# Weighted sums of chunk 8 issued with those of chunks 9 to 11, with three exponential buffers

## Chip, core and metric

One Trainium2 chip, one of its NeuronCores. The metric is the device time of one execution in microseconds (us). The time before is the median of three runs. Engines: TensorE (PE; its weight loads PEld), VectorE (DVE), ScalarE (ACT), GpSimd (POOL), SyncE (SP, which issues the transfers).

## What is computed

A decoder layer for 32 sequences of 56 tokens with 128 features: self-attention (softmax over the query axis, then the upper triangle), layer norm; cross-attention to a context of 1500 rows of 96 features with 16 heads of 8 features; layer norm; a mixture of 8 experts; layer norm. The change is in the cross-attention:

```python
q = (query @ Wq + bq).reshape(B, Nq, H, D).transpose(0, 2, 1, 3)       # 32, 16, 56, 8
k = (key_value @ Wk + bk).reshape(B, Nkv, H, D).transpose(0, 2, 1, 3)  # 32, 16, 1500, 8
v = (key_value @ Wv + bv).reshape(B, Nkv, H, D).transpose(0, 2, 1, 3)
attn = jnp.einsum('bhqd,bhkd->bhqk', q, k) * scale
attn = jax.nn.softmax(jnp.clip(attn, -CLAMP, CLAMP), axis=-1)
x = jnp.einsum('bhqk,bhkd->bqhd', attn, v).reshape(B, Nq, Cq)
```

## The kernel before

Each engine has its own program, written out by hand; they meet at semaphores alone. The cross-attention takes one batch after another. A batch is a period of twelve slots, one for each chunk of 125 of its 1500 context rows (`NC` = 12), and in the slots of batch b other work for the batches b+1 and b+2 is interleaved, by tables at the top of the file. In slot c TensorE issues, in this order:

- the scores of chunk c of batch b (line 1056, four matmuls into two banks): context rows by 16 heads x 56 queries. It needs the exponential of chunk c-2, which frees the two banks;
- the maximum pieces of `EARLY_PIECES` (line 1042): a batch has 21 pieces of 128 (head, query) rows by 500 context rows, from which VectorE takes the maxima (line 738). Piece 0 has a bank of its own, the others alternate between two, so piece n waits until VectorE has reduced piece n-2 (line 1040). Pieces 0 to 8 are those of batch b+2 and stand in slots 8 to 11, the others those of batch b+1;
- in slot 0 the sum of weights of the batch before, spread over the rows (line 1069); in slots 9, 11 and 3 values (line 1081), in slots 5, 6 and 8 keys (line 1090), all through one bank that ScalarE empties (lines 587, 588 and 571);
- the pieces of `MID_PIECES`, in slot 8 the transpose of the maxima (line 1094);
- the weighted sums listed for the slot in `OUTPUTS` (lines 1096 to 1112): a chunk k is eight small products of its exponentials with its values (lines 1106 and 1110; the trace has two matmuls for each), written to strips of 32 rows of one bank. A chunk's sum waits for its exponential (line 1103) and counts up `outputs_made`;
- the pieces of `LATE_PIECES`.

In slots 8 to 11 the pieces are: 0 and 1 in slot 8, 2 and 3 in slot 9, 4 and 5 in slot 10 (before and behind the sums), 6, 7 and 8 in slot 11 (8 behind the sums).

ScalarE takes in slot c the exponential of chunk c (line 561) into one of three buffers (`NP` = 3). Buffer c mod 3 held chunk c-3, so that it first waits for that chunk's sum, and then makes its other copies of the slot; in slot 0 the copy of the finished sums (line 556) goes ahead of the exponential:

```python
act.wait_ge(F["scores_made"], b * NC + (c + 1) + PRIME)
if not (isinstance(b, int) and b == 0 and c < NP):
    act.wait_ge(F["outputs_made"], b * NC + (c + 1 - NP) + PRIME)
```

VectorE reduces the pieces in their order and between them does the small steps of the softmax (reciprocals, line 765; scaling, line 770; a check sum, line 775). SP moves keys, queries' extra rows and context between the buffers; POOL spreads queries and makes the low parts of the keys. Batches -2 to 1 and 28 to 32 are written out, the others are a loop of two batches.

Of the kernel before, what the change touches and what calls it, by code (L numbers as in the profile page):

```python
# [51 lines left out]
EARLY_PIECES = {0: (9,), 1: (10,), 2: (11,), 3: (12,), 4: (14,), 6: (18,), 7: (20,), 9: (2,), 10: (4,), 11: (6,)}  # L52
MID_PIECES = {3: (13,), 5: (15, 16), 6: (19,), 8: (0,), 9: (3,), 11: (7,)}
LATE_PIECES = {5: (17,), 8: (1,), 10: (5,), 11: (8,)}
OUTPUTS = {2: (0, 1), 5: (2, 3, 4), 8: (5, 6, 7), 10: (8,), 11: (9, 10, 11)}
NP = 3
SLOTS = 4
FC = FF // 128
# [17 lines left out]
def decoder_kernel(nc, gate_rows, x, ctx_in, wq, wk, wv, xWq, xbq, xWk, xbk, xWv, xbv, xWo, xbo, Wr, W1, W2, out):  # L76
# [8 lines left out]
    with stack:  # L85
# [230 lines left out]
        def has(b, ahead):  # L316

            return not isinstance(b, int) or 0 <= b + ahead < B
# [635 lines left out]
        def _(pe):  # L954
# [90 lines left out]
            def period(b, par, half):  # L1045
                for c in range(NC):
# [48 lines left out]
                    if has(b, 0):  # L1095
                        for k in OUTPUTS.get(c, ()):
                            if k == 0:
# [196 lines left out]
```

## Time and profile before

| | us |
|---|---|
| median of 3 runs | 1089.12 |
| lowest and highest run | 1088.51, 1092.87 |
| the profiled execution, its own time | 1091.83 |
| its span (first to last instruction) | 1090.1 |
| TensorE busy in it | 1000.2 (92%) |
| mean granted TensorE clock, of full speed | 0.931 |

The page gives busy time by engine, the span in 40 slices of 27.25 us, and the chain of work that ended last. A line of the timeline is: start in us from the span's start, length in us, engine, line of the program, operation, what is written and read, shape, how many instructions are merged in it, and in brackets how long the engine was idle before it and what ended that. L1042 is line 1042 of the program. The cross-attention runs from about 65 to 822 us.

### The profile page before, as it was taken

The page shows a single profiled execution, that of the slowest core. Times are in us where ns is not written, and L with a number is a line of the kernel's source. Part 1 is how long each engine was busy: PE and PEld are TensorE (multiplying, and loading weights), DVE is VectorE, ACT ScalarE, POOL GpSimd, SP SyncE. Part 2 cuts the span into 40 slices and gives each one's busy share as a digit, 9 for nine tenths or more (in the row PEclk, how much of TensorE's full clock was granted, in tenths as well). Part 3 has the DMA queues.
Part 4 walks back from the last instruction along what each step waited for, and adds up shares of the span by engine and source line. Part 5 has one row for each costly group of instructions (what it writes and reads, how often), then busy time and mean ns, then how long its engine had stood idle before and what let it go on. Part 6 is the DMA issues. An engine that isn't in the chain of part 4 may idle for free.

```text
span 1090.1 us, 29459 instructions
## 1 busy us (share of the span) xinstructions
PE 1000.2 (92%) x10672; PEld 803.6 (74%) x10672; DVE 769.0 (71%) x1525; ACT 630.9 (58%) x994; POOL 355.1 (33%) x325
## 2 busy tenths in 40 slices
PE   6578999999999999999999999999986978999993
PEld 5345777777777777777777777777865867888993
DVE  3766777777777777777777777777732257677996
ACT  3204776777767777767776677776760023344551
POOL 7324332233332233322333322333100051125852
PEclk9757999999999999999999999999996559899997
DMA  4068556665456654566644566545511010003401
GB/s 93 0 136 178 108 108 143 138 140 110 106 125 141 138 125 106 110 142 139 138 106 106 130 141 137 121 106 114 130 36 41 1 39 0 20 21 124 154 34 34
DMA packets 41431, 109.57 MB, mean 101 GB/s; under 512 B 15075, under 2 KB 23590, under 8 KB 41382
## 3 DMA queue, kind: packets, MB, share of 16 engines
q1 hardware_dynamic: 41382, 108.93, 44.6%
q8 instruction: 29, 0.48, 0.2%
q14 instruction: 20, 0.16, 0.0%
HBM read 31.32 MB, written 0.97 MB: 30 GB/s over the span
## 4 chain that ended last, share of the span: by engine, by line
PE 73%; issue 9%; DVE 9%; POOL 4%; SPq 2%; DMA 2%; ACT 1%; DVEq 0%; POOLq 0%; ACTq 0%
PE psum L1042 15%; PE psum L1056 14%; PE psum L1106 11%; PE psum L1090 7%; PE psum L1081 5%; PE psum L1110 4%; PE psum L1173 3%; POOL OS_all L516 3%; DVE arena L738 3%; PE psum L1201 2%; PE psum L1202 1%; PE psum L1203 1%; PE psum L1069 1%; PE psum L1174 1%; PE psum L1212 1%
## 5 line engine op out<-in xcount | busy, mean ns | idle before, releaser
L738 DVE TENSOR_REDUCE arena<-psum 128x1 f32<-128x500 f32 x672 | 443.1, 671 | 178.2 <-PE psum L1042 178.0
L561 ACT ACTIVATE arena<-psum 125x896 f32<-125x896 f32 x384 | 348.0, 916 | 124.0 <-PE psum L1056 115.9
L1042 PE MATMUL psum<-K_hi,Q_bd 128*128 128x500 f32 x672 | 324.8, 494 | 23.8 <-DVE arena L738 21.0
L460 POOL TENSOR_TENSOR arena<-arena,K_hi 128x500 fp32r<-128x500 f32 x96 | 124.1, 1293 | 397.3 <-ACT K_hi L573 395.9
L1056 PEld LDWEIGHTS psum<-Q_st,K_st 97*125 97x125 f32 x1536 | 221.3, 189 | 30.9 <-issue 11.4
L1056 PE MATMUL psum<-Q_st,K_st 97*125 97x224 f32 x1536 | 241.0, 280 | 2.8 <-issue 1.7
L1042 PEld LDWEIGHTS psum<-K_hi,Q_bd 128*128 128x128 f32 x672 | 130.0, 195 | 80.0 <-DVE arena L738 38.7
L1106 PE MATMUL psum<-arena 125*25 125x168 f32 x3072 | 170.0, 311 | 0.2
L620 ACT ACTIVATE K_st<-psum 128x448 fp32r<-128x448 f32 x128 | 69.7, 545 | 88.8 <-PE psum L1203 88.4
L1110 PE MATMUL psum<-arena 125*9 125x56 f32 x3072 | 117.4, 213 | 0.0
L1110 PEld LDWEIGHTS psum<-arena 125*9 125x9 f32 x3072 | 94.3, 91 | 16.0
L1081 PEld LDWEIGHTS psum<-WvA,arena 97*125 97x125 f32 x768 | 102.6, 193 | 4.0
L1081 PE MATMUL psum<-WvA,arena 97*125 97x128 f32 x768 | 103.1, 278 | 0.0
L1090 PE MATMUL psum<-arena,WkA 97*128 97x500 f32 x186 | 96.7, 602 | 0.6 <-ACT arena L571 0.6
L850 DVE SCALAR_TENSOR_TENSOR K_st<-psum,K_st 128x448 fp32r<-128x448 f32 x128 | 76.2, 618 | 27.2 <-ACT K_st L620 26.1
L1106 PEld LDWEIGHTS psum<-arena 125*25 125x25 f32 x3072 | 69.2, 103 | 33.8 <-issue 25.7
L479 POOL TENSOR_TENSOR Q_st<-arena,four_heads 96x896 fp32r<-96x896 f32 x32 | 53.7, 1678 | 101.9 <-PE psum L1056 80.9
L571 ACT COPY arena<-psum 128x500 f32<-128x500 f32 x93 | 53.8, 578 | 40.9 <-PE psum L1042 21.6
L587 ACT COPY arena<-psum 125x384 f32<-125x384 f32 x96 | 46.7, 487 | 41.4 <-PE psum L1081 41.4
L765 DVE RECIPROCAL arena<-psum 128x112 f32<-128x112 f32 x64 | 53.8, 843 | 20.9 <-PE psum L1069 20.9
L573 ACT CAST K_hi<-arena 128x500 fp32r<-128x500 f32 x93 | 56.6, 609 | 3.0
L472 POOL TENSOR_TENSOR Q_bd<-Qt_all,head_rows 128x896 fp32r<-128x896 f32 x32 | 54.6, 1709 | 1.9 <-DVE Qt_all L717 1.8
(248 smaller groups left out, 1152.7 us busy)
## 6 DMA issues: line engine op xcount, KB each, us to landing
K_st<-K_hi SPq DMA_DIRECT2D x256, 187.5 KB, 4.7
K_st<-arena SPq DMA_DIRECT2D x128, 187.5 KB, 3.4
arena<-in_ctx SPq DMA_DIRECT2D x32, 562.5 KB, 6.7
arena<-gate_rows SPq DMA_DIRECT2D x8, 896.0 KB, 4.3
arena<-in_L_ffn_W SPq DMA_DIRECT2D x16, 256.0 KB, 3.5
Q_st<-max_row SPq DMA_DIRECT2D x224, 0.5 KB, 1.7
arena<-K_st SPq DMA_DIRECT2D x12, 224.0 KB, 4.9
out<-x_all SPq DMA_DIRECT2D x4, 224.0 KB, 2.5
```

The lines of the kernel that those rows point to most:

```text
L460: g.tensor_tensor(low.bitcast(F32R), low, K_hi[:, par, n * KB:n * KB + KB].bitcast(F32), ALU.subtract).then_inc(F["keys_low"], 1)
L561: a.activation(P2[c % NP].rearrange("p (n k) -> p n k", n=2), psum[0:CK, 2 + 2 * (c % 2):4 + 2 * (c % 2), 0:HQ // 2], ACT.Exp)\
L573: a.copy(K_hi[:, par, n * KB:n * KB + KB], K_lo[:, n * KB:n * KB + KB]).then_inc(F["keys_high"], 1)
L620: a.activation(h_hi[k % 2][:, f], bank[f][:, 0:QC], ACT.Relu).then_inc(S4["hidden_high"], 1)
L738: v.reduce_max(mx[:, n // NB, n % NB:n % NB + 1], bank_of(n)[:, 0:KB], AX.X).then_inc(F["piece_max_taken"], 1)
L850: v.scalar_tensor_tensor(h_lo[k % 2][:, f], bank[f][:, 0:QC], 0.0, h_hi[k % 2][:, f].bitcast(F32), ALU.max, ALU.subtract)\
L1042: mm(bank_of(n)[:, 0:KB], Q_bd[:, p].rearrange("p h q -> p (h q)")[:, 128 * (n // NB):128 * (n // NB) + 128], K_hi[:, p, (n % NB) * KB:(n ...
L1056: last = mm(bank[2 + 2 * (c % 2) + g // 2][0:CK, 4 * S * (g % 2):4 * S * (g % 2) + 4 * S], K_st[0:DC + 1, par, g, c * CK:c * CK + CK], Q_s ...
L1081: last = mm(bank[7][0:CK, 128 * k:128 * k + 128], ctxT2[:, (par + ahead) % 2, CK * q:CK * q + CK], WvA[:], start=True, stop=True)
L1090: mm(bank[7][:, 0:KB], WkA[:], ctxT2[:, par, n * KB:n * KB + KB], start=True, stop=True).then_inc(F["keys_made"], 1)
L1106: mm(bank[6][32 * m:32 * m + V3, 0:3 * S], values[:, k, V3 * m:V3 * m + V3], weights_[:, 3 * S * m:3 * S * m + 3 * S], start=(k == 0), sto ...
L1110: last = mm(bank[6][32 * m:32 * m + V1, 3 * S:4 * S], values[:, k, 4 * V3 + V1 * m:4 * V3 + V1 * m + V1], weights_[:, (12 + m) * S:(13 + m ...
```

## The change

One entry of a table. Chunk 8's weighted sums are issued in slot 11, ahead of those of chunks 9 to 11, and no longer in slot 10. The groups of sums in a batch are then those of slots 2, 5, 8 and 11. `NP` stays 3, and so do ScalarE's waits.

```diff
--- before.py
+++ after.py
@@ -52,7 +52,7 @@
 EARLY_PIECES = {0: (9,), 1: (10,), 2: (11,), 3: (12,), 4: (14,), 6: (18,), 7: (20,), 9: (2,), 10: (4,), 11: (6,)}
 MID_PIECES = {3: (13,), 5: (15, 16), 6: (19,), 8: (0,), 9: (3,), 11: (7,)}
 LATE_PIECES = {5: (17,), 8: (1,), 10: (5,), 11: (8,)}
-OUTPUTS = {2: (0, 1), 5: (2, 3, 4), 8: (5, 6, 7), 10: (8,), 11: (9, 10, 11)}
+OUTPUTS = {2: (0, 1), 5: (2, 3, 4), 8: (5, 6, 7), 11: (8, 9, 10, 11)}
 NP = 3
 SLOTS = 4
```

## Rows read from the trace of the kernel before

**Rows 1.** The page: busy time; granted clock in 40 slices.

```profile
PE 1000.2 (92%) x10672; PEld 803.6 (74%) x10672; DVE 769.0 (71%) x1525; ACT 630.9 (58%) x994; POOL 355.1 (33%) x325
...
PEclk9757999999999999999999999999996559899997
```

**Rows 2.** Line 1094 in the whole span: nanoseconds min/median/max, first and last start.

```profile
L1094 PE MATMUL psum<-ident,arena x64: 272/275/417, 89.1 to 797.8; 128*7 128x128 f32 x64
```

**Rows 3.** Timeline of TensorE, slots 10 and 11 of one batch and the next slot.

```profile
505.86 0.49 PE L1042 MATMUL psum<-K_hi,Q_bd 128*128 128x500 f32 x1 [0.58 <-DVE arena L738]
506.27 0.49 PE L1106 MATMUL psum<-arena 125*25 125x168 f32 x8
...
506.79 0.50 PE L1042 MATMUL psum<-K_hi,Q_bd 128*128 128x500 f32 x1
507.12 0.60 PE L1056 MATMUL psum<-Q_st,K_st 97*125 97x224 f32 x4
507.56 0.39 PE L1042 MATMUL psum<-K_hi,Q_bd 128*128 128x500 f32 x1
507.79 1.04 PE L1081 MATMUL psum<-WvA,arena 97*125 97x128 f32 x8
...
508.99 0.49 PE L1106 MATMUL psum<-arena 125*25 125x168 f32 x8
...
509.39 0.47 PE L1106 MATMUL psum<-arena 125*25 125x168 f32 x8
...
509.77 0.47 PE L1106 MATMUL psum<-arena 125*25 125x168 f32 x8
...
510.27 0.49 PE L1042 MATMUL psum<-K_hi,Q_bd 128*128 128x500 f32 x1
...
511.48 0.35 PE L1069 MATMUL psum<-arena,sum_rows 128*128 128x224 f32 x1
```

**Rows 4.** Waits of TensorE (all) and ScalarE (one), 100 to 800 us: us, times, longest.

```profile
PE psum L1042 <- DVE arena L738: 16.1, 28, 0.6
PE psum L1094 <- DVE arena L749: 0.6, 1, 0.6
...
ACT arena L561 <- PE psum L1110: 2.4, 2, 1.2
```

**Rows 5.** Timeline of VectorE, same batch: pieces 3 and 4.

```profile
505.72 1.33 DVE L738 TENSOR_REDUCE arena<-psum 128x1 f32<-128x500 f32 x2
```

**Rows 6.** Timeline of ScalarE, same batch: slot 11 and the copy of the sums.

```profile
507.76 0.92 ACT L561 ACTIVATE arena<-psum 125x896 f32<-125x896 f32 x1 [1.53 <-PE psum L1056]
508.86 0.49 ACT L587 COPY arena<-psum 125x384 f32<-125x384 f32 x1 [0.19 <-PE psum L1081]
...
510.48 0.35 ACT L556 COPY arena<-psum 128x224 f32<-128x224 f32 x1 [0.96 <-PE psum L1110]
```

**Rows 7.** Timeline, batches 30 and 31: waits between the sums and the exponentials.

```profile
804.92 0.67 PE L1056 MATMUL psum<-Q_st,K_st 97*125 97x224 f32 x4 [1.74 <-issue]
...
811.67 0.49 PE L1106 MATMUL psum<-arena 125*25 125x168 f32 x8
...
812.38 0.92 ACT L561 ACTIVATE arena<-psum 125x896 f32<-125x896 f32 x1 [0.58 <-PE psum L1110]
...
817.30 2.62 ACT L561 ACTIVATE arena<-psum 125x896 f32<-125x896 f32 x3 [0.39 <-PE psum L1056]
...
818.89 0.49 PE L1106 MATMUL psum<-arena 125*25 125x168 f32 x8
...
819.97 0.49 PE L1106 MATMUL psum<-arena 125*25 125x168 f32 x8
```

**Rows 8.** Batch 31: TensorE's timeline, and busy time, clock (PEclk) of that stretch.

```profile
807.22 0.78 PE L1106 MATMUL psum<-arena 125*25 125x168 f32 x8
...
807.96 0.79 PE L1106 MATMUL psum<-arena 125*25 125x168 f32 x8
...
807.20:810.60 3.40, 3.40 (x41) 2.77 (x40) 0.94 (x4) 1.57 (x3) 0.00 (x0) 0.50 0.02 5
```

## The prediction

> **What bounds the kernel now.** I read the page first: TensorE is busy 92% of the span, VectorE 71%, ScalarE 58% [rows 1]. So the attention stage is a queue of TensorE work, and the question is in which order it can be fed. The batches follow each other every 22.9 to 23.1 us: the transpose of the maxima (two matmuls a batch) is there 64 times between 89.1 and 797.7 us [rows 2]. One batch is representative of all.
>
> Then I read TensorE's timeline over slots 10 and 11 of one batch [rows 3]. In order: maximum piece 4 (505.86), weighted sum of chunk 8 (506.27), piece 5 (506.79), scores of chunk 11 (507.12), piece 6 (507.56), values (507.79), the sums of chunks 9, 10 and 11 (508.99, 509.39, 509.77), piece 8 (510.27), and in the next slot the sum row (511.48). Two things are to be seen. A chunk inside a group has a pitch of 0.38 us; the lone chunk 8 costs 506.79 - 505.86 = 0.93 us from piece to piece, where a piece and its successor of the same kind are 0.23 apart (507.56 to 507.79). And the list of waits says that in 28 batches TensorE stands 0.57 us on average before a maximum piece until VectorE has read an earlier one [rows 4]; piece 4 is that piece. VectorE's own timeline shows that the backlog goes on behind it: pieces 3 and 4 are reduced without a pause from 505.72 [rows 5].
>
> Last, ScalarE's timeline [rows 6]: the exponential of chunk 11 starts at 507.76, as soon as its scores exist, and is over by 508.68, before TensorE comes to the group at 508.99. It can start then because chunk 8's sum, which read the same one of three buffers, was over in slot 10.
>
> **The change, part by part.** No instruction is added or removed. Eight small matmul pairs (chunk 8) move behind the scores of chunk 11, piece 6, the values and piece 7. SP's, POOL's and VectorE's programs are the same.
>
> *Removed: one entry into the sums and one exit.* From rows 3 the lone chunk costs 0.93 - 0.38 - 0.23 = 0.32 us more than a chunk inside a group, and the scores after it start 0.33 behind piece 5 instead of 0.23: 0.42 us in all. What of it is gained depends on the next wait. The Trainium skill ("TensorEngine Tiling (Array Packing)", Tiling Modes, Key Properties) says that changing the tiling mode drains TensorE; the sums write 32-row strips and the pieces do not, and by that rule alone the change would give these 0.42 us back 32 times.
>
> *What is late next in slot 10: VectorE.* Piece 5 takes the bank that piece 3 had, and may start only when piece 3 has been reduced. Piece 3's reduction starts at 505.72 and takes 0.67 (rows 5: two in 1.33), so it ends at 506.39; TensorE follows about 0.05 later. Without chunk 8 in between, TensorE would be ready at 505.86 + 0.23 = 506.09 and stands until 506.44. So piece 5 comes 506.79 - 506.44 = 0.35 us earlier, not the 0.70 that the freed time would give. Piece 6 waits for piece 4, which is reduced back to back and ends at 507.05, so it could start from 507.10; it would come at 507.56 - 0.35 = 507.21, and is not held. The group starts at 508.99 - 0.35 = **508.64**.
>
> *Added: a wait on ScalarE's side, and one on TensorE's behind it.* The exponential of chunk 11 must now wait for the sum of chunk 8, which is the first chunk of the same group. How long after the group's start does such an exponential begin? The last batch shows that very pattern, where ScalarE has nothing else to do: group at 811.67, exponential at 812.38, its wait ended by line 1110 [rows 7]. That is 0.71 us. So it starts at 508.64 + 0.71 = 509.35 and, at 0.92 us [rows 6], ends at 510.27. TensorE meanwhile does chunks 9 and 10 and reaches chunk 11 at 508.64 + 0.40 + 2 x 0.38 = 509.80. It has to stand until the exponential is ready. The handover is also in rows 7: three exponentials end at 817.30 + 2.62 = 819.92, and TensorE starts the chunk behind the last at 819.97, 0.05 later. So chunk 11 starts at **510.32**, after a stall of 0.52 us, and piece 8, 0.52 behind the start of a chunk that begins alone (506.27 to 506.79), at **510.84**. Before it was 510.27. **Net: +0.57 us per batch.** Checked by parts: 0.35 gained, one chunk's 0.38 moved in, 0.52 of standing, and a fresh start of the last chunk (0.02).
>
> *Who is behind ScalarE's wait.* In its queue stand the copies of the values (started at 508.86, the first 0.49) and the copy of the sums (0.35, at 510.48) [rows 6]. They now follow at 510.27: the two value copies, at no more than 0.49 each, end by 511.25, the sums' copy follows the start of the last chunk by 0.71 (509.77 to 510.48), so it starts at 511.03 to 511.25 and ends by 511.60. The sum row needs both, and comes at 511.48 + 0.57 = 512.05. So some 0.45 us of cover hides this; without it the rest would be added to the batch. The next batch's first exponential waits for scores that are 0.57 later too. VectorE has one piece less to catch up with and waits longer. POOL's and SP's work has its triggers in scores and maxima that come 0.35 earlier or 0.57 later, and costs nothing: in 700 us TensorE's list of waits holds only maxima of VectorE and no transfer [rows 4], so what comes at most 0.57 later stays hidden.
>
> *How many batches.* The maxima of the batch after next make slots 8 to 11 full in batches 0 to 29. Piece 4 stands in 28 of them; in the other two TensorE is not held there, but VectorE's order is the same, and I take the same price: 30 x 0.57 = 17.1. Batch 30 has no pieces and ends before a wait of 1.74 us for the next batch's inputs (804.92, [rows 7]); its delay of 0.6 disappears in it. In batch 31 the end is open: chunk 11 goes from 819.97 to about 818.89 + 0.71 + 0.92 + 0.05 = 820.57, +0.6. **Sum: +17.7 us.** Against the profiled execution (span 1090.10, its own time 1091.83) that is 1109.5; that execution is 2.7 over the median of the three runs, 1089.12, to which I forecast **1106.8**.
>
> *Bounds.* The price of the wait: if ScalarE reacts as it does to scores (0.04 after their end) and not as in rows 7, a good 0.06 less; if the pause costs TensorE a full entry from another kind of work (0.41 instead of 0.23 ahead of the chunk), 0.18 more. Piece 5: at least 0, if it comes no earlier than now, at most 0.70. With the first two alone the price is 0.5 to 0.76 per batch, or 1105 to 1112. I let the low end go to 1100, for a stall that the turn into the next slot partly absorbs (0.36 per batch).
>
> **Rivals.** *No stall (same).* If the exponential of chunk 11 were ready when TensorE gets to it, four chunks would end 1.28 + 0.38 = 1.66 behind 508.64, at 510.30 against 510.27: +0.03 per batch, +1 us in all, 1090. It decides at one point: whether three chunks last as long as release, exponential and handover, 0.71 + 0.92 + 0.05 = 1.68. They last 1.16. At a granted clock of 0.50 (1.2 GHz) they would last longer: from 807.22 to 807.96 the pitch is 0.74, thrice that 2.2, after TensorE had stood for 1.74 [rows 7, 8]. But the granted clock is 9 tenths or more in all 25 slices from 109 to 790 us [rows 1], with TensorE's 0.57 of standing in each batch, and the two waits of 0.35 and 0.52 are shorter than that. Chance 0.05.
>
> *The switch is gained whole (faster).* One fewer change between kinds of matmul, nothing late behind it: 32 x 0.42 = 13.4 us, 1075.7. It needs both waits absent, VectorE's on piece 5 and ScalarE's. Against it stand the reductions back to back in rows 5 and the buffer count. The drain rule is the page's; the trace agrees on the drain (0.93 against 0.61) and not on the sum. Chance 0.05, with milder forms of it 0.06.
>
> *Nothing gained in slot 10 (slower still).* If VectorE's backlog moves with the work and piece 5 is no earlier than today, the price is 0.57 + 0.35 = 0.92, 30 x 0.92 = 27.6, 1117. Against: VectorE's reductions of pieces 3 and 4 do not hang on chunk 8. Chance 0.04.
>
> *The edit does not do what it says.* The table alone decides where TensorE issues a sum; ScalarE's waits count sums by chunk. I see no way for it; it would read as no change and is inside that chance.
>
> **How the numbers follow.** Forecast (a net stall of some half microsecond in 30 batches) 0.85, slower still 0.04, no change 0.05, faster 0.06. A measurement of this kernel can tell about 0.5%, 5.4 us, from no change. So slower 0.89, same 0.05, faster 0.06. The range is the forecast's own, 1100 to 1112: what is outside it is the rivals' 0.15 and little more.
>
> **What the profile after would show.** Right: sums 32 x 8 pairs in four groups a batch; a gap of 0.5 us inside the last, ahead of its fourth chunk, ended by line 561; exponential 11 waits for line 1110, some 30 times more than the 2 of now [rows 4]; piece 5 held by VectorE for 0.35; period up by 0.57. Wrong: fourth chunk without a gap, or a period within 0.1 of 23.0; piece 5 straight behind piece 4 (then VectorE was not late); or a new wait at the sum row, which would say that ScalarE's queue had no cover.

## The result, and the profile after

The changed kernel takes 1108.49 us in the median of four runs (1107.36 to 1109.06), against 1090.99 for the kernel before, measured beside it on the same chip (1088.51 to 1094.87). The ratio is 1.0156, with a 95% interval from 1.0123 to 1.0189: slower by some 17 us. The profiled execution took 1108.92, with a span of 1107.2 against 1090.1.

| | before | after |
|---|---|---|
| span, us | 1090.1 | 1107.2 |
| a batch, mean from the transpose of batch 1 to that of batch 28 | 23.00 | 23.63 |
| end of the cross-attention (last sum row), us | 821.7 | 839.8 |
| all that comes behind it | 268.4 | 267.4 |

The whole loss is in the cross-attention. The page of the changed kernel, busy time and the chain by engine and by line (to be read against rows 1):

```profile
PE 1002.0 (91%) x10672; PEld 801.6 (72%) x10672; DVE 764.4 (69%) x1525; ACT 627.1 (57%) x994; POOL 354.6 (32%) x325
...
PE 69%; DVE 10%; issue 9%; POOL 4%; ACT 4%; SPq 2%; DMA 2%; DVEq 0%; POOLq 0%; ACTq 0%
```

The same work in the same instructions, and a longer span: ScalarE stands in the chain with 4%, where the page of before gave it 1%. The transposes are still 64 and end 19 us later (to be read against rows 2):

```profile
L1094 PE MATMUL psum<-ident,arena x64: 272/274/417, 89.4 to 816.6; 128*7 128x128 f32 x64
```

TensorE's timeline of the batch that stands in rows 3 (its transpose at 511.98, there at 501.11). A row "x2" is two pieces that follow each other, here 4 and 5:

```profile
516.73 1.08 PE L1042 MATMUL psum<-K_hi,Q_bd 128*128 128x500 f32 x2 [0.58 <-DVE arena L738]
517.64 0.59 PE L1056 MATMUL psum<-Q_st,K_st 97*125 97x224 f32 x4
518.08 0.41 PE L1042 MATMUL psum<-K_hi,Q_bd 128*128 128x500 f32 x1
518.32 1.04 PE L1081 MATMUL psum<-WvA,arena 97*125 97x128 f32 x8
519.12 0.47 PE L1042 MATMUL psum<-K_hi,Q_bd 128*128 128x500 f32 x1
519.51 0.49 PE L1106 MATMUL psum<-arena 125*25 125x168 f32 x8
...
520.30 0.47 PE L1106 MATMUL psum<-arena 125*25 125x168 f32 x8
...
521.20 0.49 PE L1106 MATMUL psum<-arena 125*25 125x168 f32 x8 [0.33 <-ACT arena L561]
...
521.72 0.49 PE L1042 MATMUL psum<-K_hi,Q_bd 128*128 128x500 f32 x1
522.29 0.69 PE L1056 MATMUL psum<-Q_st,K_st 97*125 97x224 f32 x4
```

The group starts at 519.51, its first three chunks have a pitch of 0.40 and 0.38, and the fourth starts 0.90 behind the third, released by the exponential. The bracket says 0.33 and not 0.52 because the bar of the third chunk reaches on into the standing time. ScalarE's timeline of the same stretch (to be read against rows 6), then VectorE's (rows 5):

```profile
520.23 0.92 ACT L561 ACTIVATE arena<-psum 125x896 f32<-125x896 f32 x1 [3.13 <-PE psum L1110]
521.04 0.48 ACT L587 COPY arena<-psum 125x384 f32<-125x384 f32 x1
521.40 0.29 ACT L588 COPY arena<-psum 125x128 f32<-125x128 f32 x1
521.92 0.34 ACT L556 COPY arena<-psum 128x224 f32<-128x224 f32 x1 [0.23 <-PE psum L1110]
```

```profile
514.58 1.50 DVE L775 TENSOR_TENSOR arena<-arena 128x1 f32<-128x1 f32 x1
516.01 3.19 DVE L738 TENSOR_REDUCE arena<-psum 128x1 f32<-128x500 f32 x5
```

ScalarE has been idle for 3.13 us when chunk 8's sum (line 1110) lets it take exponential 11, 0.72 behind the group's start. VectorE reduces five pieces without a pause. The waits of the changed kernel from 100 to 810 us (to be read against rows 4):

```profile
PE psum L1042 <- DVE arena L738: 16.1, 28, 0.6
PE psum L1106 <- ACT arena L561: 9.9, 30, 0.3
...
ACT arena L561 <- PE psum L1110: 92.0, 30, 3.1
```

VectorE's wait is what it was; 30 new ones have come, one for each of batches 0 to 29. Measured from the batch's transpose, in the medians of 25 batches: piece 4 at 4.73 before and 4.74 after, piece 5 at 5.67 and 5.32, the last group at 7.87 and 7.53, piece 8 at 9.15 and 9.73.

### The profile page after: what moved, and what is told of

It is laid out like the page before. It is cut to its first block, busy times and chain, and to the rows that moved or that the text cites. A ratio compares the mean times of both kernels' runs of the same rounds, so it can differ in the third digit from the quotient of the medians.

```text
span 1107.2 us, 29459 instructions
## 1 busy us (share of the span) xinstructions
PE 1002.0 (91%) x10672; PEld 801.6 (72%) x10672; DVE 764.4 (69%) x1525; ACT 627.1 (57%) x994; POOL 354.6 (32%) x325
## 4 chain that ended last, share of the span: by engine, by line
PE 69%; DVE 10%; issue 9%; POOL 4%; ACT 4%; SPq 2%; DMA 2%; DVEq 0%; POOLq 0%; ACTq 0%
PE psum L1042 14%; PE psum L1056 14%; PE psum L1106 10%; PE psum L1090 7%; PE psum L1081 5%; DVE arena L738 4%; PE psum L1110 3%; ACT arena L561 3%; PE psum L1173 3%; POOL OS_all L516 3%; PE psum L1201 1%; PE psum L1202 1%; PE psum L1203 1%; PE psum L1069 1%; DMA arena<-gate_rows 1%
```

## Experiments

The theory: exponential 11 needs the buffer of chunk 8, whose sum is now the first of the very group that ends with chunk 11, so ScalarE and TensorE wait for each other in turn. The rival: chunk 8's work was moved from a place where VectorE held TensorE anyway to one where nobody waits, and its own time is the loss. Beyond that: what is a saved group worth, and why did it bring nothing here? All ratios are against the kernel before on the same chip.

### A fourth buffer

```diff
 OUTPUTS = {2: (0, 1), 5: (2, 3, 4), 8: (5, 6, 7), 11: (8, 9, 10, 11)}
-NP = 3
+NP = 4
```

> The changed kernel with a fourth exponential buffer (one number). Theory A: the loss is ScalarE's wait for the buffer that chunk 8 holds. With a fourth buffer exponential 11 waits for chunk 7, done in slot 8, so the gap of 0.3 us on the matmul row (0.5 us of standing) inside the last group goes, the waits of line 1106 on line 561 fall from 30 to 0, and piece 8 comes at 0.03 behind its place of before: 30 x 0.03 = +1 us against the kernel before (1090 to 1093). Rival B: the loss is chunk 8's work itself, moved from a place where VectorE held TensorE anyway to one where nothing is waiting; then the fourth buffer changes nothing and the kernel stays 17 us slower.

Measured: 1093.05 (ten runs), ratio 1.0036, interval 1.0014 to 1.0058. A batch takes 23.02 us, 0.02 more than before. TensorE's timeline of the group and its waits from 100 to 800 us:

```profile
506.73 0.49 PE L1106 MATMUL psum<-arena 125*25 125x168 f32 x8
...
507.52 0.47 PE L1106 MATMUL psum<-arena 125*25 125x168 f32 x8
...
507.90 0.47 PE L1106 MATMUL psum<-arena 125*25 125x168 f32 x8
...
508.40 0.49 PE L1042 MATMUL psum<-K_hi,Q_bd 128*128 128x500 f32 x1
```

```profile
PE psum L1042 <- DVE arena L738: 16.1, 28, 0.6
PE psum L1056 <- ACT arena L561: 0.6, 1, 0.6
```

The fourth chunk follows 0.38 behind the third, and the wait for line 561 is gone from line 1106. The rival falls. Of the time that is left over the kernel before, 0.02 us a batch explains less than 1 us; the interval starts at 1.5 us (0.14% of 1091). In its trace the stretch from batch 0's transpose to batch 30's is 0.7 us longer than before. The rest was not found in the trace.

The control, the kernel before with four buffers (`NP = 4` alone):

> The kernel before with a fourth buffer alone: the control of the run above. Theory A: no exponential of it waits on the sums on TensorE's path, so 0, within 2 us of the kernel before. Under B too. If it is faster by several us, the fourth buffer helps elsewhere and the first run has to be read against this one.

1090.89, ratio 0.9997 (0.9971 to 1.0023), 23.00 us a batch: the buffer is worth nothing without the joined group.

### What a group costs

```diff
-OUTPUTS = {2: (0, 1), 5: (2, 3, 4), 8: (5, 6, 7), 10: (8,), 11: (9, 10, 11)}
+OUTPUTS = {2: (0, 1), 5: (2, 3), 6: (4,), 8: (5, 6, 7), 10: (8,), 11: (9, 10, 11)}
```

> The kernel before with chunk 4 moved from the group of slot 5 to one of its own in slot 6: one more entry and exit per batch, in slots where VectorE holds nobody. If a switch costs what the lone chunk 8 shows in the trace, 0.32 us up to the next piece and 0.42 with the scores behind it, times 32: +10 to +13 us. If its cost is only visible beside a wait (rival), 0 to 3 us.

Measured: 1098.13, ratio 1.0104 (1.0047 to 1.0161); 23.32 us a batch, **+0.32**. So a switch has a price where nobody waits. In this place scores follow the lone chunk and not a piece, so the run does not price the arrangement of slot 10, for which I had named 0.42; the trace of the next run does.

### VectorE's check sum taken out of POOL's way

```diff
-                    if c == 8 and has(b, -1):
+                    if c == 6 and has(b, -1):
                         dve.wait_ge(F["outputs_scaled"], b + PRIME)
                         v.tensor_tensor(chk_sum, chk_sum, chk, ALU.add).then_inc(F["check_added"], 1)
```

> The kernel before with VectorE's check sum (line 775) taken in slot 6 and not in slot 8, where it ran 1.50 us instead of 0.14 beside POOL's line 472 in 28 batches. If that step is what makes VectorE late for piece 4, the wait of 0.57 goes, and the batches look like batches 0 and 29, whose piece 8 comes 8.32 us behind the transpose and not 9.15: 28 x 0.83 = 23 us faster, 1066 to 1070. If the stretch moves along with the step (it then meets line 460 of POOL) or VectorE is late from its own load, the wait stays and the gain is under 5 us.

Measured: 1067.82, ratio 0.9786 (0.9737 to 0.9836), 22.18 us a batch, 0.83 less. The check sum (line 775, from 130 to 790 us; ns min/median/max), then all waits of TensorE in that stretch:

```profile
L775 DVE TENSOR_TENSOR arena<-arena x31: 149/150/159, 131.3 to 784.3; 128x1 f32<-128x1 f32 x31
```

```profile
PE psum L1056 <- issue: 1.5, 1, 1.5
PE psum L1094 <- DVE arena L749: 0.5, 1, 0.5
PE psum L1056 <- ACT arena L561: 0.4, 2, 0.2
```

An addition of one number per partition, of 0.15 us by itself, was 1.50 long in slot 8 and made VectorE late for the pieces behind it. 28 waits of 0.57 go with it, and 0.26 a batch more than those: in medians piece 4 comes at 4.00 behind the transpose and not at 4.73 (the bar of the piece or scores before covers a part of such a wait), and piece 5 0.84 behind it and not 0.93. TensorE's timeline around the lone chunk 8, which now waits for nobody (to be read against rows 3):

```profile
469.57 0.39 PE L1042 MATMUL psum<-K_hi,Q_bd 128*128 128x500 f32 x1
469.89 0.49 PE L1106 MATMUL psum<-arena 125*25 125x168 f32 x8
...
470.41 0.50 PE L1042 MATMUL psum<-K_hi,Q_bd 128*128 128x500 f32 x1
470.75 0.60 PE L1056 MATMUL psum<-Q_st,K_st 97*125 97x224 f32 x4
```

From piece 4 to chunk 8 it is 0.32 here, and 0.41 in rows 3, where piece 4 had just stood; from piece to piece 0.84 and 0.93. Batches 0 and 29 of the kernel before, where piece 4 does not stand, have the 0.84 too. So the lone chunk costs 0.84 - 0.38 - 0.23 = 0.23 us up to the next piece, and with the 0.10 of the scores behind it 0.33 in all: the forecast's 0.42 held 0.09 that belongs to piece 4's standing and not to the switch.

### The changed kernel with the check sum moved, with three and with four buffers

> The changed kernel (three buffers) with VectorE's check sum in slot 6, so that piece 4 is held by nobody. Theory A: the stall of the last group hangs on ScalarE and the three buffers alone, so the loss is the same 0.57 to 0.62 us per batch, now against the kernel before with its check sum moved (22.18 us per batch): 22.75 to 22.80, about 1085, and line 1106 still waits 30 times for line 561. Rival: the loss came from VectorE's lateness; then it goes with it, and the batch is 22.2 us, 1068.

1084.69, ratio 0.9946 (0.9916 to 0.9977), 22.80 us a batch: 0.63 more than with the check sum moved alone. Its group, and its waits from 100 to 790 us:

```profile
460.88 0.49 PE L1106 MATMUL psum<-arena 125*25 125x168 f32 x8
...
461.67 0.47 PE L1106 MATMUL psum<-arena 125*25 125x168 f32 x8
...
462.57 0.49 PE L1106 MATMUL psum<-arena 125*25 125x168 f32 x8 [0.33 <-ACT arena L561]
```

```profile
PE psum L1106 <- ACT arena L561: 9.9, 30, 0.3
```

With VectorE's lateness gone, the price of the joined group is the same as with it (0.62): the two are independent.

With four buffers as well:

> Four groups, four buffers and the check sum in slot 6: neither of the two waits. My step for slot 10 says that piece 5 is held by the reduction of piece 3 all the same (piece 3's ends 4.45 us behind the transpose, TensorE would be ready at 4.23), so piece 5 comes at 4.49 and not 4.84, piece 8 at 8.35 against 8.32: 22.20 us per batch, 1068 to 1070, no gain from the saved switch. If the hold was only that of the late check sum, piece 5 comes at 4.23 and the batch is 0.2 us or more shorter: 1061.

1068.5, ratio 0.9804 (0.9776 to 0.9832), 22.20 us a batch, against 22.18 with five groups. From the transpose, in medians: piece 4 at 4.00, piece 5 at 4.50, piece 8 at 8.36. So with neither of the two waits in the list the saved switch is still lost, and the step says where: piece 5 stands 0.27 for the reduction of piece 3, which ends at 4.45 in the median of this trace, 0.05 ahead of piece 5. It does not show as a wait, because the bar of piece 4 covers it; only its distance of 0.50 and not 0.23 tells.

### Another order of the pieces

```diff
-EARLY_PIECES = {..., 10: (4,), 11: (6,)}
-MID_PIECES = {..., 9: (3,), 11: (7,)}
-LATE_PIECES = {5: (17,), 8: (1,), 10: (5,), 11: (8,)}
+EARLY_PIECES = {..., 10: (4,), 11: (5,)}
+MID_PIECES = {..., 9: (3,), 11: (6, 7)}
+LATE_PIECES = {5: (17,), 8: (1,), 11: (8,)}
```

on top of four groups, four buffers and the early check sum.

> As the run above, with piece 5 behind the scores of chunk 11 and piece 6 behind the values, so that no piece stands directly behind the one whose bank's predecessor is still being reduced. The saved switch should now be seen: piece 8 at about 8.00 behind the transpose and not 8.32, 0.32 us per batch, 30 x 0.32 = 10 us less than with the check sum moved alone: 1056 to 1059. If a switch costs nothing where nobody waits, it stays at 1068.

**1058.71**, ratio 0.9718 (0.9686 to 0.9751): 2.8% faster than the kernel before, and the best version found. 21.83 us a batch, 0.35 less than with the check sum moved alone. TensorE's timeline (transpose at 477.96):

```profile
481.96 0.39 PE L1042 MATMUL psum<-K_hi,Q_bd 128*128 128x500 f32 x1
482.19 0.59 PE L1056 MATMUL psum<-Q_st,K_st 97*125 97x224 f32 x4
482.62 0.40 PE L1042 MATMUL psum<-K_hi,Q_bd 128*128 128x500 f32 x1
482.86 1.04 PE L1081 MATMUL psum<-WvA,arena 97*125 97x128 f32 x8
483.65 0.70 PE L1042 MATMUL psum<-K_hi,Q_bd 128*128 128x500 f32 x2
484.29 0.49 PE L1106 MATMUL psum<-arena 125*25 125x168 f32 x8
...
485.95 0.49 PE L1042 MATMUL psum<-K_hi,Q_bd 128*128 128x500 f32 x1
```

Nothing stands: pieces 4 and 5 have the scores between them, pieces 5 and 6 the values, and piece 8 comes 7.99 behind the transpose. Two runs tell whether that is the saved group or the order. First the same with five groups:

> The fastest version so far (four buffers, check sum in slot 6, piece 5 behind the scores of chunk 11), with chunk 8 back in a group of its own in slot 10: the five groups of the kernel before. It tells the saved switch from the new order of the pieces. If the gain of 0.37 us per batch over the version with the old order came from the saved switch, it is given back: piece 8 at 8.3 and not 7.99 behind the transpose, 22.15 to 22.2 us per batch against 21.83, about 1068. If it came from the order alone, the batch stays at 21.8 and the time at 1058.

1067.4, ratio 0.9793 (0.9761 to 0.9825), 22.16 us a batch, piece 8 at 8.32. The order by itself is worth nothing (22.16 against 22.18); the saved group is worth 0.33 a batch, the 0.32 of the added one with the sign turned. Then the same four groups with three buffers:

> The fastest version so far with three buffers. If the price of the wait hangs on three buffers and four chunks in a group and on nothing else, the fourth chunk starts 1.68 behind the group and not 1.17: 0.53 to 0.60 us per batch more, 22.36 to 22.43, about 1076, with 30 waits of line 1106 on line 561.

1074.24, ratio 0.984 (0.9807 to 0.9872), 22.42 us a batch, +0.60, with 31 waits of line 1106 on line 561 up to 790 us. The stall is the same a third time.

### Three groups of four

```diff
-OUTPUTS = {2: (0, 1), 5: (2, 3, 4), 8: (5, 6, 7), 11: (8, 9, 10, 11)}
+OUTPUTS = {3: (0, 1, 2, 3), 8: (4, 5, 6, 7), 11: (8, 9, 10, 11)}
```

This edit is made to the fastest version, the one of 1058.71 with four buffers; "the run above" is that one in what follows.

> As the run above, with the twelve chunks in three groups of four (slots 3, 8 and 11). By the price of a switch alone 0.32 us per batch less again, 1047. Against it: pieces 15, 16 and 17 of slot 5 then follow each other without a group between them and wait for VectorE, 0.4 to 0.7 us. I expect no gain over the run above, within 5 us of it, with new waits of line 1042 on line 738.

A miss in size: 1094.67, ratio 1.0027 (1.0005 to 1.0049), 23.00 us a batch, 1.17 more than with four groups. From 130 to 790 us, and around piece 17:

```profile
PE psum L1042 <- DVE arena L738: 17.3, 32, 0.6
```

```profile
520.25 1.01 PE L1042 MATMUL psum<-K_hi,Q_bd 128*128 128x500 f32 x2
521.81 0.49 PE L1042 MATMUL psum<-K_hi,Q_bd 128*128 128x500 f32 x1 [0.55 <-DVE arena L738]
```

Pieces 15, 16 and 17 now follow each other and the third stands 0.55, as expected. Of the other 0.6 us the medians show the scores of slot 3 held (0.12 of idle time before them), the values of slot 3 0.40 behind their piece instead of 0.24, and the rest was not taken apart by a run.

## Why the prediction was right

By its steps, from the medians of 25 batches:

- **Piece 5 is held by VectorE and comes 0.35 earlier, not 0.70.** Measured 5.67 - 5.32 = 0.35. The runs with four buffers and with the new order show the same step from the other side.
- **The exponential starts 0.71 behind the group, the fourth chunk at 1.68, piece 8 at 2.20.** Measured in the batch shown: 0.72, 1.69, 2.21. A wait pattern of the last batch, where ScalarE had nothing else to do, gave the number for one that did not exist yet.
- **+0.57 us a batch.** Piece 8 went from 9.15 to 9.73 (+0.57 to 0.58). The batch as a whole went up by 0.62, and here a term was missing: even batches grew by 0.57 (22.90 to 23.47), odd ones by 0.66 (23.13 to 23.79). In every second batch TensorE's program turns its loop, between piece 8 and the next scores. In the batch shown that distance went from 510.72 - 510.27 = 0.45 to 0.57, in the median of the odd batches from 0.45 to 0.53. The forecast had put this at nothing, and had even let its low end go down for a turn that absorbs a part of the stall.
- **The cover behind ScalarE's wait holds.** The copy of the sums is over at 522.26, and the sum row comes 0.56 later than before in even batches (10.71 against 10.15 behind the transpose) and 0.66 later in odd ones (11.03 against 10.37), no more than what is in front of it.
- **Batch 30 swallows its delay, batch 31 does not.** TensorE stood 1.11 before batch 31's scores and not 1.74: 0.63 swallowed. The last batch's fourth chunk came 1.68 behind its group (836.46 to 838.14). TensorE's timeline of the changed kernel there:

```profile
823.71 0.67 PE L1056 MATMUL psum<-Q_st,K_st 97*125 97x224 f32 x4 [1.11 <-issue]
...
836.46 0.49 PE L1106 MATMUL psum<-arena 125*25 125x168 f32 x8
...
838.14 0.49 PE L1106 MATMUL psum<-arena 125*25 125x168 f32 x8 [0.33 <-ACT arena L561]
```

- **The sum.** Forecast +17.7; the ratio gives +17.0 (13.4 to 20.6), the spans +17.1. That the total fits so well is in part luck. In the two traces, from the transpose of batch 0 to that of batch 30 it is +18.5, where the forecast has 17.1: the 13 odd batches from 1 to 25 bring the 1.4. From there to the last sum row it is -0.7, where the forecast has +0.6, and behind it -1.0, where it has nothing; both have a stretch less at the lower clock in the changed kernel (below). The rest is 0.3 ahead of the batches.
- **The gain from the drain.** The Trainium skill ("TensorEngine Tiling (Array Packing)", Tiling Modes, Key Properties) says that a change of tiling mode drains TensorE. The runs agree that a switch costs something where the work is not held otherwise, 0.32 to 0.33 us and not the 0.42 that the prediction read; they do not tell a drain from any other cost of going from one kind of matmul to another. The rival that had this gain come through needed both waits absent. It took a fourth buffer and another order of the pieces, and in the runs also the check sum out of VectorE's way; there the saved switch brought its 0.33.
- **The rival "nothing gained in slot 10"** is refuted by the 0.35, the one of "no stall" by the 30 waits.

## What to carry to other kernels

A ring of n buffers bounds a group: if the consumer's group holds n + 1 items that go through it, the producer of the last cannot start before the first is consumed, and the group waits for release, production and handover less the time of the items between (here 1.68 - 1.17). Before joining work to save a switch, ask of each neighbour what the switched-away time was covering: here the sums stood between two pieces that must not follow each other, and the saving came out only when other useful work was put there. And look at small operations that run ten times their length: the largest gain of this study (2.1%) was one of them, with no part in the change.

## What the runs showed of the hardware beyond that

**The check sum's 1.50 us.** In the changed kernel VectorE's line 775 starts at 514.58 and ends at 516.08, with POOL's line 472 beside it, in POOL's timeline:

```profile
514.38 1.69 POOL L472 TENSOR_TENSOR Q_bd<-Qt_all,head_rows 128x896 fp32r<-128x896 f32 x1
```

It ends 0.01 behind POOL's instruction, which ran its usual 1.69. In slot 6, with none of POOL's beside it, it takes 0.15. The Trainium skill ("SBUF — State Buffer", SBUF: two separate sides) describes an exclusive lock on a port pair: when a VectorE instruction with two inputs in SBUF meets a GpSimd instruction that reads SBUF, the one that starts first has the pair for its whole length, and the other is blocked. The trace agrees: POOL's instruction started first, at 514.38, and VectorE's ended with it. So it is in all 28 batches. The reductions of the maxima, which read PSUM, keep their mean of 0.67 in all these kernels.

**A clock that fell in one kernel and not in the other.** Before the change TensorE's granted clock was 0.50 (1.2 GHz) from 807.2 us [rows 8], behind a time of standing of 1.74. After it, with 1.11 of standing at the same place, the stretch around batch 31 reads 1.00. Busy times and clock, first the kernel before, then the changed one:

```profile
807.00:810.00 3.00, 3.00 (x40) 2.27 (x39) 1.14 (x4) 1.24 (x2) 0.00 (x0) 0.54 0.02 5
```

```profile
817.00:840.00 23.00, 18.14 (x365) 14.45 (x353) 2.71 (x10) 14.80 (x18) 0.00 (x0) 1.00 0.01 2
```

From batch 31's first scores to the end of the last sum row it is 16.7 us before (804.92 to 821.66) and 16.1 after (823.71 to 839.83), although that batch has its 0.6 of stall: the lower clock had cost about 1.2, an estimate from these two. The length of the standing alone does not tell the two apart. In the trace of the changed kernel with four buffers TensorE stands 1.11 at that place too, and the clock reads 0.50 from 805.0 to 808.4; in that of the kernel with one more group it stands 1.34 and the clock stays at 1.00. What decides it was not found.

Behind the attention it is the same. Besides one long stretch right behind it and the last 15 us, the kernel before has a clock of 0.50 there for 3.4 us from 906.2 and 6.8 us from 926.7, the changed one for 3.4 us from 923.5 and 3.4 us from 1002.0, and it takes 1.0 less for the same work. Of the twelve traces of this case, the eight with 10.2 us of such stretches take 268.4 to 269.4 us behind the last sum row, and the four with 6.8 us take 266.9 to 267.4.

**The loop turn.** An odd batch takes TensorE 0.23 us more than an even one before the change (23.13 against 22.90), 0.32 after it (23.79 against 23.47), 0.19 with four buffers (23.12 against 22.93, and 0.16 with the early check sum as well, 22.28 against 22.12). It is the turn and not the odd batch: batches 1 and 27 of the kernel before, behind which no turn stands, take 22.90 and 22.92, and the whole difference lies around the first scores behind piece 8. It is dearest in the kernels where TensorE has just stood for ScalarE ahead of the turn (0.32, 0.32 and 0.28, against 0.15 to 0.23 in the others). Why was not tested.
